# Both layer norms of a two-layer graph block moved from VectorE to ScalarE, as x times 1/std minus mean/std

## What is computed

```python
def _layernorm(x, axis=-1, eps=1e-05):
    m = jnp.mean(x, axis=axis, keepdims=True)
    v = jnp.var(x, axis=axis, keepdims=True)
    return (x - m) / jnp.sqrt(v + eps)

h = jnp.maximum(_layernorm(x), 0.0)
x = x + gat(h, adj)              # layer 1: 4 heads, elu; layer 2: one head
h = jnp.maximum(_layernorm(x), 0.0)
x = x + h + einsum(h, weights) + label_bias_sum(adj)
```

## Time and profile before

| | |
|---|---|
| time, median of 3 runs | 523.26 us (522.91 to 523.29) |
| the profiled execution | 523.36 us, its span 521.6 us |
| PE busy | 488.1 us, 94% |
| DVE busy | 487.1 us, 93% |
| ACT busy | 444.9 us, 85% |
| POOL busy | 386.5 us, 74% |

### The profile page before, as it was taken

How to read it: one execution, slowest core, us unless ns; L and a number is a source line. 1 busy time by engine, 2 the same in 40 slices (tenths; PEclk the granted TensorE clock), 3 DMA queues, 4 the chain that set the end, 5 groups by cost and what they waited for, 6 DMA issues and landing times.

```text
span 521.6 us, 14585 instructions
## 1 busy us (share of the span) xinstructions
PE 488.1 (94%) x3428; PEld 420.0 (81%) x3428; DVE 487.1 (93%) x1437; ACT 444.9 (85%) x1604; POOL 386.5 (74%) x556
## 2 busy tenths in 40 slices
PE   4498999999999999999999999999999999999875
PEld 1377788888888888888888888888888888888764
DVE  7989999999999999999999999999999999999763
ACT  2378999989999999999999999999999999998841
POOL 3276878878787788887777788878777887877642
PEclk9999999999999999999999999999999999999997
DMA  8110101111110111111101111111011111000011
GB/s 237 37 32 8 33 27 53 54 34 53 51 48 24 51 51 51 46 36 51 51 23 49 51 51 51 31 51 51 23 49 51 51 51 33 20 24 21 23 42 41
DMA packets 29148, 23.72 MB, mean 45 GB/s; under 512 B 1976, under 2 KB 28860, under 8 KB 29120
## 3 DMA queue, kind: packets, MB, share of 16 engines
q1 hardware_dynamic: 27328, 21.44, 13.4%
q10 hardware_dynamic: 1792, 1.98, 1.4%
HBM read 14.56 MB, written 8.39 MB: 44 GB/s over the span
## 4 chain that ended last, share of the span: by engine, by line
PE 47%; DVE 23%; issue 16%; POOL 6%; ACT 5%; ACTq 1%; DVEq 1%; POOLq 0%
DVE hn L704 8%; PE pA L913 6%; PE pY L925 4%; PE pY L926 4%; PE pY L927 4%; PE pA L906 3%; POOL P L345 3%; ACT L L441 3%; DVE nmax L734 3%; DVE L L729 3%; PE pC L950 3%; PE pH L867 2%; PE pZ L898 2%; PE pF L969 2%; PE pZ L895 2%
## 5 line engine op out<-in xcount | busy, mean ns | idle before, releaser
L446 ACT ACTIVATE L<-L,nmax 128x128 f32<-128x128 f32 x256 | 100.1, 406 | 8.8 <-DVE nmax L734 8.8
L329 POOL TENSOR_TENSOR h_lo<-h,h_hi 128x512 fp32r<-128x512 f32 x64 | 83.0, 1297 | 17.3 <-ACT h_hi L500 17.3
L352 POOL TENSOR_TENSOR hT_lo<-hT_f,hT_hi 128x256 fp32r<-128x256 f32 x64 | 47.3, 739 | 42.8 <-ACT hT_hi L429 42.6
L925 PE MATMUL pY<-w_hi,h_hi 128*128 128x258 f32 x256 | 76.5, 299 | 0.9 <-POOL h_lo L329 0.6
L926 PE MATMUL pY<-w_lo,h_hi 128*128 128x258 f32 x256 | 72.6, 283 | 0.0
L927 PE MATMUL pY<-w_hi,h_lo 128*128 128x258 f32 x256 | 72.5, 283 | 0.0
L345 POOL TENSOR_TENSOR P<-L,rsum 128x512 f32<-128x512 f32 x64 | 66.5, 1039 | 6.3 <-DVE rsum L738 6.3
L913 PE MATMUL pA<-PT,xl 128*128 128x128 f32 x512 | 67.6, 275 | 0.5 <-ACT PT L454 0.5
L704 DVE TENSOR_SCALAR hn<-x_all,mv,rstd 128x256 f32 (+1 forms) x64 | 64.5, 1007 | 2.1
L913 PEld LDWEIGHTS pA<-PT,xl 128*128 128x128 f32 x512 | 62.9, 192 | 0.7 <-ACT PT L454 0.7
L446 ACT ACTIVATION_READ_ACCUMULATOR L<-L,nmax 128x1 f32 x256 | 52.2, 204 | 0.0
(11 more groups left out here) (156 smaller groups left out, 1735.7 us busy)
## 6 DMA issues: line engine op xcount, KB each, us to landing
x_all<-in_x SPq DMA_DIRECT2D x32, 256.0 KB, 2.8
out<-x_all SPq DMA_DIRECT2D x32, 256.0 KB, 2.2
adj_all<-in_adj SPq DMA_DIRECT2D x32, 128.0 KB, 2.6
x_all<-in_L_gnn_W ACTq DMA_DIRECT2D x2, 512.0 KB, 5.4
rhs<-lhs SPq DMA_DIRECT2D x64, 6.0 KB
rhs<-lhs SPq DMA_DIRECT2D x64, 1.0 KB
x_all<-in_L_gnn_weights ACTq DMA_DIRECT2D x2, 256.0 KB, 7.7
x_all<-in_L_gnn_att_src ACTq DMA_DIRECT2D x1, 128.0 KB, 6.1
```

The lines of the kernel that those rows point to most:

```text
L329: pool.tensor_tensor(h1_lo[p][:, :, :].rearrange("p a b -> p (a b)"), h1[p][:, :], h1_hi[p][:, :, :].rearrange("p a b -> p (a b)").bitcast ...
L446: last = act.activation(L1[p][:, h, :], L1[p][:, h, :], ACT.Exp, bias=nmax1[p][:, h:h + 1], accum_out=sum1[p][:, h:h + 1])
L925: pe.matmul(pY[:, 0:C2], h1_hi[p][:, k, :], w2_hi[:, k, :], start=(k == 0), stop=False)
```

## The change

The two stages `layer_norm1` and `layer_norm2` go from DVE's list to ACT's, to the places behind `scaled2` and ahead of `exp1`; their lags (-2 and 5) stay. ACT computes Identity(scale * x + bias) with scale = 1/std and bias = `shift` = minus mean/std, both tiles with one number for each partition. For `shift`, POOL gets two products in each of `inverse_std1` and `inverse_std2`: mean times -1 ahead of the power, and the result times `rstd` behind it, behind a wait for the power (new semaphores `s_rs1b`, `s_rs2b`). The signal that the norm waits for (`s_rs1`, `s_rs2`) now comes after the last product. One `memset` for the column of -1 is added. All other stages, lags and orders stay. Declarations are left out of the diff.

```diff
@@ -305,6 +308,7 @@
             pool.memset(ident[:, :], 0.0).then_inc(s_ident, 1)
             pool.memset(off_diag[:, :], NEG).then_inc(s_ident, 1)
             pool.memset(minus_half[:, :], -0.5).then_inc(s_ident, 1)
+            pool.memset(minus_one2[:, :], -1.0)
             pool.memset(eps_col[:, :], EPS).then_inc(s_ident, 1)
             pool.wait_ge(s_ident, 4)
             pool.affine_select(out=ident[:, :], in_=ident[:, :], compare_op=ALU.not_equal, fill=1.0,
@@ -313,14 +317,18 @@
                                base=0, pattern=[[-1, 128]], channel_multiplier=1).then_inc(s_ident, 1)
 
             def inverse_std1(g, p):
+
                 if p % 2:
                     return
                 pool.wait_ge(s_mv1, g + 2)
                 if after(g, 4):
                     pool.wait_ge(s_hn, g - 2)
-                pool.tensor_tensor(ve1[:, p:p + 2], mv1[:, p:p + 2, 1], eps_col[:, :], ALU.add).then_inc(s_rs1a, 2)
+                pool.tensor_tensor(ve1[:, p:p + 2], mv1[:, p:p + 2, 1], eps_col[:, :], ALU.add)
+                pool.tensor_tensor(shift1[:, p:p + 2], mv1[:, p:p + 2, 0], minus_one2[:, :], ALU.mult).then_inc(s_rs1a, 2)
                 pool.wait_ge(s_rs1a, g + 2)
-                pool.tensor_tensor(rstd1[:, p:p + 2], ve1[:, p:p + 2], minus_half[:, :], ALU.pow).then_inc(s_rs1, 2)
+                pool.tensor_tensor(rstd1[:, p:p + 2], ve1[:, p:p + 2], minus_half[:, :], ALU.pow).then_inc(s_rs1b, 2)
+                pool.wait_ge(s_rs1b, g + 2)
+                pool.tensor_tensor(shift1[:, p:p + 2], shift1[:, p:p + 2], rstd1[:, p:p + 2], ALU.mult).then_inc(s_rs1, 2)
 
             def split_h1(g, p):
                 pool.wait_ge(s_h1hi, g + 1)
@@ -334,9 +342,12 @@
                 pool.wait_ge(s_mv2, g + 1)
                 if after(g, 2):
                     pool.wait_ge(s_h2n, g - 1)
-                pool.tensor_tensor(ve2[p][:, :], mv2[p][:, 1:2], eps_col[:, 0:1], ALU.add).then_inc(s_rs2a, 1)
+                pool.tensor_tensor(ve2[p][:, :], mv2[p][:, 1:2], eps_col[:, 0:1], ALU.add)
+                pool.tensor_tensor(shift2[p][:, :], mv2[p][:, 0:1], minus_one2[:, 0:1], ALU.mult).then_inc(s_rs2a, 1)
                 pool.wait_ge(s_rs2a, g + 1)
-                pool.tensor_tensor(rstd2[p][:, :], ve2[p][:, :], minus_half[:, 0:1], ALU.pow).then_inc(s_rs2, 1)
+                pool.tensor_tensor(rstd2[p][:, :], ve2[p][:, :], minus_half[:, 0:1], ALU.pow).then_inc(s_rs2b, 1)
+                pool.wait_ge(s_rs2b, g + 1)
+                pool.tensor_tensor(shift2[p][:, :], shift2[p][:, :], rstd2[p][:, :], ALU.mult).then_inc(s_rs2, 1)
 
             def normalise1(g, p):
                 pool.wait_ge(s_rsum1, g + 1)
@@ -419,6 +430,20 @@
                 act.activation(of_graph(mask_all, g, N), of_graph(adj_all, g, N), ACT.Relu, bias=1.0, scale=-1.0,
                                accum_out=of_graph(n0_all, g, 1)).then_inc(s_n0, 1)
 
+            def layer_norm1(g, p):
+                act.wait_ge(s_rs1, g + 1)
+                if after(g, 2):
+                    act.wait_ge(s_T0, g - 1)
+                act.activation(hn[p][:, :], of_graph(x_all, g, D), ACT.Identity, bias=shift1[:, p:p + 1],
+                               scale=rstd1[:, p:p + 1]).then_inc(s_hn, 1)
+
+            def layer_norm2(g, p):
+                act.wait_ge(s_rs2, g + 1)
+                if after(g, 2):
+                    act.wait_ge(s_T2, g - 1)
+                act.activation(h2n[p][:, :], of_graph(x_all, g, D), ACT.Identity, bias=shift2[p][:, :],
+                               scale=rstd2[p][:, :]).then_inc(s_h2n, 1)
+
             def relu_h(g, p):
                 act.wait_ge(s_T0, g + 1)
                 if after(g, 2):
@@ -524,7 +549,7 @@
                 act.wait_ge(s_w2dma, 64)
                 act.activation(w2_hi[:, :, 0:D], w2_f[:, :, :], ACT.Copy).then_inc(s_w2hi, 1)
 
-            pipeline(act, [(scaled2, 4), (exp1, 1), (exp2, 4), (high_w1, -3), (high_w2, 0), (elu_exp, 2), (score_rows2, 3), (copy_b1, -1),
+            pipeline(act, [(scaled2, 4), (layer_norm1, -2), (layer_norm2, 5), (exp1, 1), (exp2, 4), (high_w1, -3), (high_w2, 0), (elu_exp, 2), (score_rows2, 3), (copy_b1, -1),
                            (score_rows1, -1), (scaled1, 0), (high_h1, 2), (no_edges, -5), (copy_PT2, 4), (relu_h2, 5),
                            (features2, 3), (copy_PT1, 1), (relu_h, -2), (place_label_rows, 3)])
@@ -697,20 +722,6 @@
                 link(dve.tensor_reduce(top_row[:, :], pX[0:1, 0:128], AX.X, ALU.max))
                 dve.tensor_copy(top_int[:, :], top_row[:, :]).then_inc(s_label, 1)
 
-            def layer_norm1(g, p):
-                dve.wait_ge(s_rs1, g + 1)
-                if after(g, 2):
-                    dve.wait_ge(s_T0, g - 1)
-                dve.tensor_scalar(hn[p][:, :], of_graph(x_all, g, D), mv1[:, p, 0:1], rstd1[:, p:p + 1],
-                                  ALU.subtract, ALU.mult).then_inc(s_hn, 1)
-
-            def layer_norm2(g, p):
-                dve.wait_ge(s_rs2, g + 1)
-                if after(g, 2):
-                    dve.wait_ge(s_T2, g - 1)
-                dve.tensor_scalar(h2n[p][:, :], of_graph(x_all, g, D), mv2[p][:, 0:1], rstd2[p][:, :],
-                                  ALU.subtract, ALU.mult).then_inc(s_h2n, 1)
-
             def low_rows1(g, p):
                 dve.wait_ge(s_rows1, g + 1)
                 dve.tensor_tensor(lhs1[p][LO:LO + ROWS1, :], pH[0:ROWS1, 0:128], lhs1[p][0:ROWS1, :].bitcast(F32),
@@ -799,8 +810,8 @@
                 dve.tensor_tensor(of_graph(x_all, g, D), pF[:, 0:D], of_graph(x_all, g, D), ALU.add).then_inc(s_out, 1)
 
             pipeline(dve, [(weigh_w2_dst, 0), (max2, 4), (high_scores2, 3), (zero_counts, 3), (take_off_excess, 2), (low_scores2, 3),
-                           (weigh_w1_src, -2), (features1, 1), (layer_norm2, 5), (sum_w3, 1), (recip2, 4), (recip1, 1),
-                           (elu_max, 2), (normalise2, 4), (low_rows1, -1), (layer_norm1, -2), (release1, -4), (leaky1, 0),
+                           (weigh_w1_src, -2), (features1, 1), (sum_w3, 1), (recip2, 4), (recip1, 1),
+                           (elu_max, 2), (normalise2, 4), (low_rows1, -1), (release1, -4), (leaky1, 0),
                            (aggregate1, -4), (residual2, 7), (max1, 0), (residual1, 4), (weigh_w1_dst, -2),
                            (largest_labels, 3), (split_w3, 3), (weigh_w2_src, -2), (stats2, 4), (release2, 4),
                            (label_terms, 2), (stats1, -5), (aggregate2, 4), (leaky2, 3), (largest_of_rows, 3),
```

More of the change, by code:

```diff
@@ L127, in gat_graphconv_block @@
         minus_half = sb("minus_half", [128, 2])
+        minus_one2 = sb("minus_one2", [128, 2])
         eps_col = sb("eps_col", [128, 2])
@@ L204, in gat_graphconv_block @@
         rstd1 = sb("rstd1", [128, TURN])
+        shift1 = sb("shift1", [128, TURN])
         bn2 = two("bn2", [128, 6])
@@ L208, in gat_graphconv_block @@
         rstd2 = two("rstd2", [128, 1])
+        shift2 = two("shift2", [128, 1])
         pX = pb("pX", [128, 512])
@@ L228, in gat_graphconv_block @@
         s_w2sum, s_less = sem("w2_summed"), sem("excess_known")
-        s_bn1, s_mv1, s_rs1a, s_rs1, s_hn = (sem(n) for n in ("bn1_done", "mv1_done", "rs1a", "rs1", "hn_done"))
+        s_bn1, s_mv1, s_rs1a, s_rs1b, s_rs1, s_hn = (sem(n) for n in ("bn1_done", "mv1_done", "rs1a", "rs1b", "rs1", "hn_done"))
         s_n0, s_mask, s_xb = sem("n0_done"), sem("mask_done"), sem("x_biased")
@@ L239, in gat_graphconv_block @@
             sem(n) for n in ("R2", "rows2_sb", "z2", "scaled2", "leaky2", "max2", "exp2", "rsum2_done", "P2_done"))
-        s_P2T, s_PT2, s_attn2, s_x2, s_bn2, s_mv2, s_rs2a, s_rs2, s_h2n = (
-            sem(n) for n in ("P2T", "PT2_sb", "attn2", "x2", "bn2_done", "mv2_done", "rs2a", "rs2", "h2n_done"))
+        s_P2T, s_PT2, s_attn2, s_x2, s_bn2, s_mv2, s_rs2a, s_rs2b, s_rs2, s_h2n = (
+            sem(n) for n in ("P2T", "PT2_sb", "attn2", "x2", "bn2_done", "mv2_done", "rs2a", "rs2b", "rs2", "h2n_done"))
         s_T2, s_h2hi, s_h2lo, s_fin, s_out, s_stored = (
```

## The result

The changed kernel takes 695.54 us (median of 3 runs, 695.51 to 696.36) against 523.26: a ratio of 1.331, 95% interval 1.329 to 1.333. The forecast was 679 in a range of 645 to 714.

A forecast was written before the change was run, and what follows sets the result against it. Bound before: DVE's order and PE; after: a once-a-slot loop through DVE's aggregate2, POOL and ACT's norms. 523.4 + 3 (lead-in) + 143.2 (57 slots of 9.0 or 10.9) + 9 (tail) = 679 us, range 645 to 714.

The forecast's parts named there:

- The loop: aggregate2, POOL's chain, ACT's norms, exp1, then either low_h or DVE's next aggregate2: run once a slot, 9.0 or 10.9 us.
- The signs it named: Profile after: ACT's longest waits at its norms, ve2 starts alternating near 9.0 and 10.9 us, DVE about 60% busy.
- The short slot: Slot where norm 1's inverse was made the slot before: 9.0 us from ve2 to ve2, through ACT and POOL.
- the norm's step: Time one norm adds on ACT: 0.45 us, bounds 0.26 and 0.52.
- The long slot: Slot where ACT meets norm 1 first and its inverse comes from POOL after norm 2's: 10.9 us.
- The clock: PE's granted clock, forecast to stay 1.00 in the profile after.
- Rival (d): PE's clock falls because PE stands idle 26% of a slot: some +70, 750 us; chance 5%.
- Lead-in and tail: Added time outside the steady slots: 3 us before them (0 to 5), 9 us after (7 to 10).
- The steady stretch: 57 slots, 29 short and 28 long: 566.2 us against 422.98, +143.2.
- POOL's products: Two per norm, before and after rstd; first starts 0.15 us after ve2, norm 2's second done at 1.24.
- Rival (c): Faster: DVE relieved, ACT never stands at its norms, PE's 7.32 us a graph the floor: 517 us; chance 2%.
- L779 alone stretched: Sign in the profile after: L779 is the only DVE instruction left that POOL stretches; own time estimated at 0.3 us.

The follow-up runs named there:

- Experiment 1: Changed kernel with both norms later in ACT's list, behind scaled1 instead of ahead of exp1, all work the same: 547.81 us.
- experiment 7: Changed kernel plus 14 useless 128x128 matmuls in PE's pause of each long slot: 687.88 us (ratio 1.318).
- experiment 4: Changed kernel without POOL's four products, the bias given to ACT being the mean itself: 662.84 us.
- experiment 9: Kernel before plus POOL's four products, norms on DVE in their old places as x times rstd plus shift: 552.41 us (ratio 1.055).
- Experiment 12: Kernel before with one edit, normalise1 ahead of low_h2 in POOL's list, no products: 508.38 us (ratio 0.972).
- experiments 11: Kernel before with only norm 1 on ACT, behind high_h1, its shift from one small DVE instruction for two graphs: 562.41 us (ratio 1.078).
- experiments 6: Changed kernel plus 22 useless 128x128 matmuls in PE's pause of each long slot: 713.07 us (ratio 1.362).

## Why the prediction held, point by point

**The loop** was the right mechanism. Experiment 1 is the proof: same work, other place, 148 of the 172 us gone. The signs it named are there: DVE at 58% busy (forecast 60), ACT's waits at its norms (1.47 us at norm 2, 3.53 at norm 1; forecast 1.9 and 3), alternating slots. PE is at 79% and ACT at 71% where 74 and 80 were forecast; the 80 doesn't follow from the prediction's own terms, since 444.9 us and 128 norms of 0.45 are 74% of 679.

**The short slot**, 9.0 forecast, is 9.02. By its terms: ACT begins norm 2 1.34 us after `ve2` (1.30), the norm's step is 0.51 (0.45), `exp1` to the end of the last `relu_h` 6.39 (6.40), `low_h` and `ve2` 0.78 (0.81).

**The long slot**, 10.9 forecast, is 11.23 in the slot shown. `rstd1` at 1.67 (1.69) and its product done at 2.70 (2.73) were right; ACT began norm 1 only 0.22 us behind that, where one semaphore of 0.06 was assumed (it is 0.12 at norm 2 in the short slot shown), and the two norms took 1.00 instead of 0.90: `exp1` at 3.92 instead of 3.69. `exp1` to `relu_h` took 6.46, and `low_h` followed after 0.16, not 0.07. Of the 0.33 us that are missing, ACT's late start at norm 1 is 0.13, the norms are 0.10, and the way through `relu_h` and `low_h` is the rest. The norm's step of 0.50 instead of 0.45 is mis-sized in both slots; the two rows that it was taken from, L506 and L454, read PSUM, and the norms read SBUF. The estimate of 0.49 from the Trainium skill, page "ScalarE: Activation LUTs", section "What ACT_TABLE_LOAD costs", was the better one, and the trace agrees with it as a whole: worked out from it, an estimate, a norm takes 585 ns, and the medians are 603 and 599. Its 93 ns for a bias tile is not the 65 ns that the prediction read as agreement.

**The clock** "stays 1.00": wrong. Rival (d) had the mechanism, PE's pause, at 5%, and the wrong price: 7 to 8 us by experiment 7, not 70. In 19 of the 28 long slots PE restarts at full clock, and a slow stretch that comes later lies where PE has slack. The step that failed was the row it leaned on, 46% busy at full clock in the earlier trace rows: that row says how much PE worked, not how long it paused at a time. The forecast had no term for the clock, and that the time is inside the range all the same is in part luck: the room below 714 was meant for dearer steps and for PE's waits.

**Lead-in and tail.** The first `ve2` starts at 58.10, 4.1 us later than before (forecast 3); the last six periods take 43.5 us, 7.9 more (forecast 9). The steady stretch was forecast at 566.2 and took 582.5: this is the miss of 16 us. Some 10 us of it are the clock's (experiment 7's stretch takes 572.8), above all the nine slots of 12 us; the rest is 28 long slots of 11.1 even at full clock instead of 10.9 and 29 short ones longer by 0.02, some 6 us.

**POOL's products** were priced rightly in the loop: the first starts 0.14 us after `ve2` (forecast 0.15), `shift2` is done at 1.22 (forecast 1.24), and experiment 4 gives 33 us for all four. What the text lacks is their cost where no loop waits: it names `normalise1` nowhere, and experiment 9 gives 29 us for it.

**Rival (c)**, faster, took PE's 7.32 us busy a graph as a floor and so 517 us as the best. Experiment 12 runs at 7.14 a graph, with the same matmuls. PE's busy time in the trace of before was thus no floor: over the whole span it is 488.1 us there and 478.3 in experiment 12, for 3428 instructions in both; L935, for one, averages 249 ns and 226. Weight loads, 258.6 us of 300 before and 268.2 in experiment 12, had shown the room. The Trainium skill, page "Trainium Kernel Development and Optimization", section "Performance Expectations", says as much, that matmul busy time is a bad metric for the distance to the roofline and that busy weight loads are a good one; the trace agrees.

**L779 alone stretched**: not so. It (L790 after) takes 0.28 us in all 64 instances, also where it starts just before POOL's `normalise1` ends (259.34 beside 258.48 to 259.52). The forecast took the order of the two for unchanged; in the slot of the earlier trace rows L779 starts 0.08 us after POOL's `normalise1` does (249.15 against 249.07), after the change 0.86 us behind it. Its own time, 0.28, is the 0.3 that the prediction had estimated.

## What to carry to other kernels

Before work is moved to an engine with free time, compare when its input is ready with when that engine reaches the place: an in-order list turns a late input into a loop, and the same work was 548 or 696 us by its place alone. An engine that is 74% busy can still have no slack at one place; there the order of its list is worth trying before its load, and here swapping two stages gave 2.8% without any change of work. Where an instruction has a duration much over its minimum, look at what runs beside it, here POOL beside DVE (experiments 11 and 12).

## What the hardware showed that was not expected

- A 128x2 DVE instruction took 1.21 us instead of 0.15 beside a 128x512 GpSimd instruction of 1.26, and ended with it. L704's median was 0.72 us before and 0.42 when it no longer ran beside that instruction.
- After a PE pause of 3.44 us the granted clock was still 1.00 when PE worked again (260.0 to 260.5), then 0.50 from about 261.4 to 264.7; around the pause of 3.34 us in the next long slot it fell at about 278.5, before PE worked again at 279.85. Against the filled slots of experiment 7 the first slot is 0.06 us longer, the second 0.9.
- A matmul of f32 128x128 by 128x128 stands in the trace as two records and took 0.23 us for the pair in experiments 6 and 7, more than the filling had been sized by.
